# Layer-1 score products as two 64-row head pairs, and the chain between two attentions by 512-token halves

## What is computed

```
x = layernorm(x + attention0(x))   # 8 heads of 16, causal; a geo term per head from the first 3 features
y = x + mla(rmsnorm(x))            # 16 heads of 8, causal; K, V from a layer-normed latent of 64; rope on Q, K
out = layernorm(x + y + moe(rmsnorm(y)))   # 4 experts of 512 hidden (relu), one picked by a gate
```

## Time and profile before

| | us |
|---|---|
| median of three runs | 679.21 |
| lowest and highest | 676.43 and 685.65 |
| the profiled execution | 684.45 |
| its span from first to last instruction | 682.7 |
| mean granted clock of PE | 0.93 of 2.4 GHz |
| PE / DVE / ACT / POOL busy | 604.6 / 412.7 / 338.0 / 144.0 |

### The profile page before, as it was taken

One profiled execution on the slowest core, in us unless ns is written; L12 is line 12 of the kernel. 1 busy time (PEld: TensorE's weight loads), 2 busy tenths in 40 slices (PEclk: granted clock), 3 DMA queues, 4 the chain that ended last, 5 costly groups with the idle time before them and its releaser, 6 DMA issues.

```text
span 682.7 us, 10113 instructions
## 1 busy us (share of the span) xinstructions
PE 604.6 (89%) x3694; PEld 282.8 (41%) x3717; DVE 412.7 (60%) x1031; ACT 338.0 (50%) x621; POOL 144.0 (21%) x180
## 2 busy tenths in 40 slices
PE   5578899958798878889999999999989999899994
PEld 3323233424233224333433344455544555357663
DVE  3586988795603967897778787845657401422313
ACT  4234457634445434546766666645546554633330
POOL 3812212312344022125330202211002001101000
PEclk9889999968658998999999999999999999989998
DMA  4855120000035121031231221030000000000000
GB/s 142 205 175 186 33 75 22 2 1 0 28 75 96 21 43 22 1 64 45 63 49 32 33 45 21 17 48 1 2 0 17 0 2 1 17 0 1 16 1 15
DMA packets 27394, 27.69 MB, mean 41 GB/s; under 512 B 6289, under 2 KB 22545, under 8 KB 27090
## 3 DMA queue, kind: packets, MB, share of 16 engines
q1 hardware_dynamic: 26962, 26.26, 16.2%
q0 software_dynamic: 384, 0.79, 0.5%
HBM read 19.40 MB, written 7.34 MB: 39 GB/s over the span
## 4 chain that ended last, share of the span: by engine, by line
PE 67%; DVE 19%; DMA 4%; ACT 3%; issue 3%; POOL 1%; SPq 1%; DVEq 0%; ACTq 0%; POOLq 0%
PE ps L863 14%; PE ps L846 12%; PE ps L936 10%; DVE mparts L1225 10%; PE ps L823 9%; PE ps L992 8%; PE ps L925 3%; PE ps L919 3%; PE ps L820 2%; ACT pr L1012 2%; PE ps L900 2%; PE ps L874 2%; PE ps L934 2%; DMA qs<-nparts 1%; DVE stats L1135 1%
## 5 line engine op out<-in xcount | busy, mean ns | idle before, releaser
L1012 ACT ACTIVATE pr<-ps 128x512 f32<-128x512 f32 (+1 forms) x456 | 250.6, 576 | 239.3 <-PE ps L846 236.6
L1225 DVE TENSOR_REDUCE mparts<-ps 128x1 f32<-128x512 f32 (+3 forms) x456 | 280.0, 656 | 116.1 <-PE ps L823 114.9
L846 PE MATMUL ps<-qs,ks 99*128 99x512 bf16 (+3 forms) x576 | 174.6, 344 | 12.0 <-ACT pr L1012 6.0
L823 PE MATMUL ps<-ks,qs 96*128 96x512 bf16 (+3 forms) x576 | 170.8, 338 | 15.6 <-DVE mparts L1225 12.7
L740 POOL TENSOR_SCALAR_AFFINE_SELECT pr<-pr 128x512 f32<-128x512 f32 x96 | 60.9, 635 | 370.4 <-ACT pr L1012 370.2
L863 PE MATMUL ps<-pr,vs 128*32 128x512 f32 (+3 forms) x1152 | 131.3, 530 | 0.0
L846 PEld LDWEIGHTS ps<-qs,ks 99*128 99x128 bf16 x576 | 51.0, 100 | 148.6 <-ACT pr L1012 83.9
L823 PEld LDWEIGHTS ps<-ks,qs 96*128 96x128 bf16 x576 | 55.7, 101 | 54.0 <-DVE mparts L1225 21.2
L936 PE MATMUL ps<-w,work 128*128 128x128 f32 x512 | 74.1, 288 | 0.0
L820 PE MATMUL ps<-cmask,identb 128*128 128x128 bf16 (+2 forms) x241 | 58.0, 241 | 17.3 <-DVE mparts L1225 8.9
L1077 ACT ACTIVATE work<-ps,b 128x512 f32<-128x512 f32 x64 | 43.8, 687 | 49.1 <-PE ps L992 48.4
(11 more groups left out here) (115 smaller groups left out, 400.0 us busy)
## 6 DMA issues: line engine op xcount, KB each, us to landing
qs<-scr1q SPq DMA_DIRECT2D x64, 64.0 KB
ks<-scr1k SPq DMA_DIRECT2D x64, 64.0 KB
qs<-scr0q SPq DMA_DIRECT2D x48, 64.0 KB, 2.3
ks<-scr0k SPq DMA_DIRECT2D x36, 64.0 KB, 2.2
scr0q<-parts SPq DMA_DIRECT2D x4, 384.0 KB, 2.9
scr0k<-parts SPq DMA_DIRECT2D x4, 384.0 KB, 3.2
scr1q<-parts SPq DMA_DIRECT2D x4, 384.0 KB, 2.5
scr1k<-parts SPq DMA_DIRECT2D x4, 384.0 KB, 2.5
```

The lines of the kernel that those rows point to most:

```text
L823: last = pe.matmul(bank[:, h, :], queries(F, KMAX, h0 + h, i * P, P), ks[0:KMAX, F % SLOTS, h0 + h, 512 * c:512 * c + w], start=not diagon ...
L846: last = pe.matmul(to[:, h, :], ks[0:KEXP, F % SLOTS, h0 + h, j * P:(j + 1) * P], queries(F, KEXP, h0 + h, qb * 512 + lo, n), start=True, ...
L1012: act.activation(pr[:, st % PSLOTS, h0:h0 + nh, 0:STEPS[st][3]], scores_at(F, v), ACT.Exp, scale=GROUPS[F][0].scale).then_inc(exped, 1)
L1225: dve.tensor_reduce(mparts[:, F % SLOTS, h0:h0 + nh, i, c], maxes_at(F, u), AX_X, ALU.max).then_inc(taken, 1)
```

## The change

**1. Pairs of 64 rows.** Both layers now have 6 products. In layer 1 they are 48 rows, with the three rows of maxima 51. Heads 0 and 1 of a group stand in partitions 0 to 63, heads 2 and 3 in 64 to 127, so that a score or maxima product uses one half of PE's rows. Units go through the heads in the order 0, 2, 1, 3 (scores) and 2, 0, 3, 1 (maxima). A unit holds at most two heads instead of four: 40 exps and 40 reduces a group instead of 38. The mask of the diagonal is added by two products of 64 rows, with a second identity and mask (`identx`, `cmaskx`, built once on POOL by `halves`). A load is 24 DMAs of 8 x 2 x 1024 instead of 16 of 8 x 4 x 1024, the rows of maxima 6 instead of 3. `ones` takes the place of `zeros` on POOL, and every load into such a slot waits for it.

**2. The chain by halves.** `between(b, i)` writes it for one half, and stands at 1.56 to 2.15 and 2.22 to 2.82 for batch 0 (before 2.21 to 3.12), at 3.56 to 4.20 and 4.22 to 5.20 for batch 1 (before 4.21 to 5.95). The rmsnorm's inverse root is computed beside the layernorm's from the same variance, so its squares, their sum and one root are gone; `hat0` on DVE writes the doubly normed x, and `x1` on POOL the layer-normed x. Group 4 is loaded by halves, and its maxima run from -0.02 to 0.84 of group 3 (before 0.4 to 0.9).

```diff
-ATT = [Attention(0, 16, [(0, 0), (0, 1), (1, 0), (1, 1), (0, 2), (2, 0)], 16 ** -0.5),
-       Attention(1, 8, [(0, 0), (0, 1), (1, 0), (1, 1), (0, 2), (2, 0), (1, 2), (2, 1)], 8 ** -0.5)]
-
-
-KMAX = 96
-KEXP = KMAX + 3
+PRODUCTS = [(0, 0), (0, 1), (1, 0), (1, 1), (0, 2), (2, 0)]
+ATT = [Attention(0, 16, PRODUCTS, 16 ** -0.5), Attention(1, 8, PRODUCTS, 8 ** -0.5)]
+HALF = P // 2
+HEADS = [0, 2, 1, 3]
+
+HALVED = range(ATT[0].groups + 1)
...
 
     out = []
     for s, (_, _, _, n, _) in enumerate(STEPS):
-        nh = min(HG, 512 // n)
-        out += [(s, h, nh) for h in range(0, HG, nh)]
+        nh = min(2, 512 // n)
+        out += [(s, h, nh) for h in HEADS if h % nh == 0]
     return out
...
     for i in range(TB):
         for c in range(i // 4 + 1):
             w = min(512, (i + 1) * P - 512 * c)
-            nh = min(HG, 512 // w)
-            out += [(i, c, h, nh, w) for h in range(0, HG, nh)]
+            nh = min(2, 512 // w)
+            out += [(i, c, (h + 2) % HG, nh, w) for h in HEADS if h % nh == 0]
     return out
...
-MAX_LATE = (0.4, 0.9)
+MAX_LATE = (-0.02, 0.84)
...
+def between(b, i):
+
+    q = block_of(1, b, 0, i)
+    k = block_of(1, b, 1, i)
+    latent = root("latent", b, (i,))
+    return [*output(0, b, (i,)), ("moments", 0, b, i), *root("x1", b, (i,)), ("hat0", b, i), ("x1", b, i),
+            ("feed", "hat0", b, i), ("feat", "hat0", b, i),
+            ("latent", b, i), ("lat_copy", b, i), ("proj", q, 0), ("lat_moments", b, i), ("rotate", q, 0),
+            ("proj", q, 1), *latent[:2], ("rotate", q, 1), *latent[2:], ("rotated", q), ("lat_norm", b, i), ("hi", q),
+            ("lat_turn", b, i), ("r1", q), ("lat_feat", b, i), ("mid", q), ("proj", k, 0), ("lo", q),
+            ("rotate", k, 0), ("store", q), ("proj", k, 1), ("rotate", k, 1), ("rotated", k),
+            ("v_proj", 1, b, i), ("hi", k), ("v_out", 1, b, i), ("r1", k), ("mid", k), ("lo", k), ("store", k)]
...
+    first = loads(0, ATT[0].groups)
+    for i in range(2):
+        out += spread(between(0, i), *BETWEEN[0][i]) + [(BETWEEN[0][i][1], step) for _, step in first[2 * i:2 * i + 2]]
+        out += spread(between(1, i), *BETWEEN[1][i])
+    out += loads(BETWEEN[0][1][1], ATT[0].groups + 1)
...
+    out += [(1.5, ("halves",))]
+    out += [(F - 2 + 0.01, ("ones", F)) for F in range(ATT[0].groups, ATT[0].groups + SLOTS)]
...
-BETWEEN = [(2.21, 3.12), (4.21, 5.95)]
+BETWEEN = [[(1.56, 2.15), (2.22, 2.82)], [(3.56, 4.2), (4.22, 5.2)]]
...
             for i in ((half,), (half,), (0, 1))[half]:
                 M = block_of(at.n, g // at.gb, k, i)
                 queue.wait_ge(stored[M % PARTS], stored_value(M))
-            if F >= SLOTS:
+            if ("ones", F) in NTH:
+                queue.wait_ge(done["ones"], 2 * nth("ones", F))
+            elif F >= SLOTS:
                 queue.wait_ge(scored, (F - SLOTS + 1) * NU)
             cols = (slice(0, T // 2), slice(T // 2, T), slice(0, T))[half]
             for j, pair in enumerate(at.products):
                 src = scr[at.n][k][pair[k]].rearrange("b c t -> (b c) t")[g * at.gw:(g + 1) * at.gw, cols]
+                if at.n == 1:
+                    for pair_of in range(2):
+                        first = HALF * pair_of + j * at.hd
+                        to = (qs, ks)[k][first:first + at.hd, F % SLOTS]
+                        to = (to[:, 0:2 * T].rearrange("p (h t) -> p h t", h=2) if k == 0 else to[:, 0:2, :])[:, :, cols]
+                        heads = src[pair_of * at.gw // 2:(pair_of + 1) * at.gw // 2, :]
+                        queue.dma_start(to, heads.rearrange("(h d) t -> d h t", d=at.hd)).then_inc(qk_in[F % SLOTS][half % 2], 16)
+                    continue
...
+                at = GROUPS[F][0]
                 for p in range(3):
-                    to, src = qs[KMAX + p:KMAX + p + 1, F % SLOTS, cols], nparts[0:n, place, p, :]
-                    if q == 2 and GROUPS[F][0].n == 0:
+                    if at.n == 1:
+                        for pair_of in range(2):
+                            row = HALF * pair_of + at.kprod + p
+                            sp.dma_start(qs[row:row + 1, F % SLOTS, 0:2 * T],
+                                         nparts[2 * TB * pair_of:2 * TB * (pair_of + 1), place, p, :]).then_inc(rows_in, 16)
+                        continue
+                    to, src = qs[at.kprod + p:at.kprod + p + 1, F % SLOTS, cols], nparts[0:n, place, p, :]
+                    if q == 2:
                         to = to.rearrange("a (c x) -> a c x", c=2)
                     sp.dma_start(to, src).then_inc(rows_in if q else rows_first, 16)
...
+            def ones(F):
 
                 pool.wait_ge(scored, (F - SLOTS + 1) * NU)
                 pool.wait_ge(*before)
-                pool.memset(qs[ATT[1].kprod:KMAX, F % SLOTS, :], 0.0).then_inc(done["zeros"], 1)
-                pool.wait_ge(done["zeros"], nth("zeros", F))
+                for first in (32, HALF + 32):
+                    pool.memset(ks[first:first + 32, F % SLOTS, 0:2, :], 1.0).then_inc(done["ones"], 1)
+                pool.wait_ge(done["ones"], 2 * nth("ones", F))
...
                 diagonal = 512 * c + w == (i + 1) * P
-                if diagonal:
+                if diagonal and GROUPS[F][0].n == 0:
                     pe.matmul(bank[:, :, w - P:w], identb[:, :], cmask[:, 0:nh, :], start=True, stop=False,
                               skip_group_check=True)
+                elif diagonal:
+
+                    own = slice(HALF * (h0 // 2), HALF * (h0 // 2) + HALF)
+                    low, high = ((identb, cmask), (identx, cmaskx))[::-1 if h0 // 2 else 1]
+                    pe.matmul(bank[:, :, w - P:w], low[0][own, :], low[1][own, 0:nh, :], start=True, stop=False,
+                              skip_group_check=True)
+                    pe.matmul(bank[:, :, w - HALF:w], high[0][own, :], high[1][own, 0:nh, HALF:P], start=False, stop=False,
+                              skip_group_check=True)
                 for h in range(nh):
-                    last = pe.matmul(bank[:, h, :], queries(F, KMAX, h0 + h, i * P, P),
-                                     ks[0:KMAX, F % SLOTS, h0 + h, 512 * c:512 * c + w],
+                    last = pe.matmul(bank[:, h, :], queries(F, 0, h0 + h, i * P, P),
+                                     keys(F, 0, h0 + h, 512 * c, w),
                                      start=not diagonal, stop=True, skip_group_check=True)
                 last.then_inc(given, 1)
...
                     pe.wait_ge(rows_in, 48)
                 if v == 0:
                     if F:
-                        pe.wait_ge(rows_in, 48 * (F + 1))
+                        pe.wait_ge(rows_in, rows_value(F))
                     else:
...
                 to = scores_at(F, v)
                 for h in range(nh):
-                    last = pe.matmul(to[:, h, :], ks[0:KEXP, F % SLOTS, h0 + h, j * P:(j + 1) * P],
-                                     queries(F, KEXP, h0 + h, qb * 512 + lo, n),
+                    last = pe.matmul(to[:, h, :], keys(F, 3, h0 + h, j * P, P),
+                                     queries(F, 3, h0 + h, qb * 512 + lo, n),
                                      start=True, stop=True)
                 last.then_inc(scored, 1)
```

211 lines of the change are left out of this document (111 added, 100 removed).

## The result

The changed kernel takes 762.2 us (median of 4 runs, 757.6 to 777.1), the kernel before beside it on the same chip 682.4: ratio 1.118, 95% interval 1.102 to 1.134. The forecast was 662. The profiled execution took 765.25 us, 763.4 of them its span, 80.7 more than the span before.

A forecast was written before the change was run, and what follows sets the result against it. PE was taken to bound clean and expert groups, waits and clock groups 2 and 3. Groups 1 to 5 -12.9, 6 to 11 -4.8, extra exps and reduces +0.5: -17.2 from 684.45, 667.3, or 662.1 by the median; range 628 to 704.

The forecast's parts named there:

- The stand: Ahead of group 3's first score: PE waits for maxima rows queued behind loads on SP, 17 us, bounds 14 and 21.
- pairs in groups 4 and 5: Groups 4 and 5: products in different row halves running at once save 8.4 us.
- mode changes and masks: Group 3: more changes between row modes and the split diagonal masks cost 6.5 us.
- I put 10 us on it and on the windows: After the wait ahead of group 3 and in the four chain windows: a clock at 1.2 GHz costs 10 us.
- half of 72.7, 36 us; ... so I take 33: Chain of one half: bounds 26 us of PE work and half the old batch 0 chain, 36; 33 taken.
- the windows then idle ... 18: The four half-chain windows: PE idles 7.5, 7, 3.5 and 0 us, 18 in all.
- together 57 us: Groups 2 to 5: PE's idle time and clock dilation that can be had back, 57 us.
- Just above DVE's 25: Clean groups: PE falls from 31.3 to 27.1 us, near DVE's 25; 1.8 us for six maxima rows makes 29.0.
- its two score banks keep its scores apart: Group 11: no maxima to pair with, so no overlap; 21 more mode changes cost 2 us at most, 1 taken.
- The first ended on the right side: Rival: SP queue wait of 20 us and 1.2 GHz through group 3; 702 us, 697 by the median; chance 0.22.
- Row pairs don't overlap: Rival: products in different row halves don't run at once, clean groups take 34.4 us, total 697; chance 0.10.
- the halves hide: Rival: windows idle 5 us, clock costs 3, clean groups 27; 636 us, 631 by the median; chance 0.22.

The follow-up runs named there:

- pairs alone: The kernel before with only the 64-row layout, units, masks, loads and rows of layer 1 changed, its chain kept: 720.8 us against 683.9.
- halves alone: The kernel before with only the new chain by halves, its places and group 4's halved loads, layer 1 keeping 96 and 99 rows: 731.4 us against 683.9.
- the streams: Series of products without other work, full rows, one half or alternating halves, with varied waits, behind the last expert product of pairs alone; 0.108 us each alternating, 0.215 one half.
- the same shorter chain: The kernel before with the second part's shorter chain steps, layer 1 in full rows, at the old places: both halves together 666.9 us, one after the other 718.8.
- the pairs on the shorter chain: The changed kernel without the halving: row pairs, and the shorter chain with both halves together at the old places; 700.5 us against 682.5.

## Why the prediction was wrong, step by step

**Right.** The overlap (0.108 us a product in pairs), and that alternating halves is free. Clean groups' work on PE, 27.1 forecast, 27.2 and 27.5 measured where they ran at full clock. The stand, 17 forecast and 16.7 measured, with its releaser. That it came so near is in part luck: its main path was `ones` 5 and the 24 loads behind it, but `ones` 5 was done in time, and it was 48 loads in a row, 17.3 us behind the last store of batch 0's K, that held the queue. Groups 9 and 10, +0.3 and -0.4 forecast, +0.7 and +0.6 measured. PE's work in groups 1 to 5 fell by 9.8 us where the terms "pairs in groups 4 and 5", "mode changes and masks" and "building on POOL" came to about -1. Group 3's +6.5 did not show: its work went from 37.3 to 38.1 with 60 more changes between row modes, so that the 0.09 us a change, read from one place, does not show there; why is open.

**Groups 1 to 5: +60.3 measured, -12.9 forecast.** Of the 73 us between them the clock has 57 and idle time 25, and less work takes 9 off. Two steps failed. The first is "I put 10 us on it and on the windows": dilation came to 66.7 us. The sum took the 26.6 us of before as had back and let the stand and the windows bring the clock down for 10 us in all. But narrow products without a partner lose it by short waits and then keep it down (pairs alone has 56.3 us of dilation with hardly more idle time than before), and the waits of 3 to 5 us that the half chains make bring it down in any rows (44.1 in halves alone), as the streams show for both.

The second is the length of a half's chain, "half of 72.7, 36 us; ... so I take 33", and with it "the windows then idle ... 18" and "together 57 us" to be had back. A half's chain took 45.0 and 50.3 us. The bound was no bound at all: it let each half have half of the hops, and a half has all of them. Idle time went from 30.6 to 60.3 us, of which 43.6 besides the stand, where I had 18. The comparison that would have shown it is the same shorter chain, 666.9 us whole and 718.8 halved at the same places.

**Clean groups: 29.0 forecast, 31.1 at full clock, 32.7 and 34.3 in the changed kernel.** "Just above DVE's 25" left out the rest of the boundary. In group 6 of the pairs on the shorter chain, work fell by 3.6 us and idle time rose by 3.4: 2.2 in the wait for the six rows (1.8 priced), and 1.4 in waits of single scores for ACT, by the view of waits, which a faster PE no longer covers. In the changed kernel dilation of 5.0 and 3.6 us came on top.

**Group 11: +1 forecast, +10.1 measured.** The prediction saw that "its two score banks keep its scores apart", and took from it only that nothing is gained. That those unpaired products can't hold the clock was not among its terms.

**The rivals.** The first ended on the right side and named the right two things, the SP queue and half clock on 64-row products with 177 to 211.2 as its sign. Its 697 was 65 us short. It had the clock in groups 3 and 4 (+30 and +10, while dilation there rose by 21.6 and 9.9), but no more idle time in the windows than the forecast, and nothing in groups 1, 2, 6 to 8 and 11. (Its 41 us of work would be 82 at half clock and not 76, which is no matter for the result.) The range left out what all priced cases shared: every one of them let halving be a gain. "Row pairs don't overlap" is refuted, "the halves hide" too.

## What to carry over

A half of a chain that crosses all engines has all of its hops, so count its length by hops and not by work: two interleaved halves of a shorter chain won 1.5%, and the same halves one after the other lost 5%. Before narrowing PE's products, ask for each stretch whether every one has a partner in the other half of the rows: without one, short waits left PE at 1.2 GHz here, and the work saved was worth less than the clock. And when steps are moved in a queue, look which DMAs now stand ahead of the ones that somebody waits for; here moving two loads gave 32 us back.

## What the runs showed of the hardware

- 51-row products in the lower half of the rows, with no wait at all between them, ran 125 us at 1.2 GHz after a pause of 7 us (0.427 us each for 512 columns); from 2.4 GHz and without a pause they held it for 54 us; with waits of 0.4 us after every 3.5 or 7 us of work they fell 5 and 8 us after their start and stayed down for the rest of 143 and 277 us. Full rows and alternating halves under the same waits never fell.
- With blocks of 7 us of full rows, waits of 1.0 us left the clock at 1.00; waits of 2.8 and 5.1 us gave a mean of 0.86 and 0.78. Alternating halves gave the same three numbers.
- Full rows kept groups 6, 7 and 11 at 1.00 in every profile that had them (31.3, 31.3 and 41.0 to 41.1 us); with narrow rows groups 6 and 7 took 31.1 to 39.0 and group 11 44.3 to 51.2. In group 11 rows of zeros were enough.
- Alternating halves: 0.108 us a product at 2.4 GHz, half of 0.215.
- A pause of 16.7 us cost 32 us where the work behind it was narrow and full of short waits, and 21 with full rows.
- The same paired code ran a clean group at 1.00 in one profile and at 0.69 in another; what decides between the two is open.
